# Two-layer attention and expert kernel: batch 1's layer norm, transposes and V matmuls made during batch 0, and GpSimd sums the rotated key in batch 1's first pass

## The reference, cut to what matters

```python
x = x + _layernorm(attn(_layernorm(x)))          # x: (2, 2048, 256), float32
x = x + _layernorm(ffn(_layernorm(x)))
# attn, cut:
xn = x * rsqrt(mean(x * x) + 1e-6) * rms_w
proj = xn @ in_proj_W.T + in_proj_b              # z, K (pairs), V; DI = 512
u = silu(conv4(V) + conv_b)                      # causal, 4 taps, per channel
# per head gates from u: a, w (rotation), beta, r_gate, u_gate, sel_B, sel_C
def step(Sc, inp):                               # scan over the tokens
    Sr = rotate(Sc, a11, a12)
    err = v - sum(k * Sr)
    return Sr + beta * err * k
y = group_norm(sum(Q * Y)) * silu(z) + D * u
return residual + y @ out_W.T
# ffn, cut: a router picks 2 of 8 experts for each batch; gelu(x @ W1 + b1) @ W2 + b2
```

## Time and profile before

| | |
|---|---|
| Median of 3 runs | 1502.98 us (1501.24 to 1503.02) |
| The profiled execution | 1502.64 us, its span 1500.8 us |
| Mean granted TensorE clock | 0.938 |
| PE busy | 1258.7 us (84% of the span), 4244 matmul instructions |
| DVE busy | 1179.0 us (79%), 1933 instructions |
| ACT busy | 516.8 us (34%) |
| POOL busy | 173.9 us (12%), 77 instructions |
| DMA | 98.73 MB, 18.8% of 16 engines' span |

### The profile page before, as it was taken

The page is one execution under the profiler, slowest core; times in us unless marked ns, Lnnn a source line. Parts: engine busy times, 40 slices in busy tenths (PEclk is TensorE's granted clock), DMA queues, the critical chain, the costliest instruction groups (busy, mean ns, idle before and its releaser), DMA issues. The chain is left out here.

```text
span 1500.8 us, 13138 instructions
## 1 busy us (share of the span) xinstructions
PE 1258.7 (84%) x4244; PEld 742.3 (49%) x4244; DVE 1179.0 (79%) x1933; ACT 516.8 (34%) x1186; POOL 173.9 (12%) x77
## 2 busy tenths in 40 slices
PE   5960887773989698895999999899997797999997
PEld 2540333331555455453666666565554474666664
DVE  5889999899999968789899999859999775610011
ACT  3762111000223364666532232321223554332332
POOL 0000244401221200000011111001222100000000
PEclk9985999996999899798999999999999898999999
DMA  4000111100311032200223331312111103432221
GB/s 169 1 8 14 57 52 47 70 1 14 110 45 57 15 118 112 64 8 0 71 84 98 98 98 56 112 70 99 43 57 42 57 1 117 140 133 70 85 70 70
DMA packets 52117, 98.73 MB, mean 66 GB/s; under 512 B 4689, under 2 KB 40018, under 8 KB 50898
## 3 DMA queue, kind: packets, MB, share of 16 engines
q1 hardware_dynamic: 52050, 97.91, 18.8%
HBM read 75.87 MB, written 22.02 MB: 65 GB/s over the span
## 5 line engine op out<-in xcount | busy, mean ns | idle before, releaser
L677 PE MATMUL ps<-kz 128*128 128x256 f32 x1024 | 243.6, 381 | 15.0 <-ACT kz L921 13.3
L663 PE MATMUL ps<-kz 128*128 128x512 f32 x512 | 244.3, 601 | 5.7 <-DVE coef L1110 5.7
L677 PEld LDWEIGHTS ps<-kz 128*128 128x128 f32 x1024 | 195.2, 191 | 98.0 <-issue 60.4
L555 PE MATMUL ps<-wshare,uT 128*128 128x512 f32 x512 | 227.4, 598 | 0.0
L921 ACT ACTIVATE kz<-ps,small 128x512 f32<-128x512 f32 x128 | 87.5, 686 | 302.3 <-PE ps L663 302.1
L477 PE MATMUL ps<-wshare,xnT 128*128 128x512 f32 x256 | 119.3, 610 | 63.4 <-ACT ps L741 63.2
L555 PEld LDWEIGHTS ps<-wshare,uT 128*128 128x128 f32 x512 | 95.9, 192 | 109.8 <-issue 109.8
L663 PEld LDWEIGHTS ps<-kz 128*128 128x128 f32 x512 | 98.5, 193 | 83.0 <-issue 71.4
L975 POOL TENSOR_TENSOR work<-work 128x1024 f32<-128x1024 f32 x28 | 66.8, 2387 | 623.7 <-DVE work L1401 388.3
L823 ACT ACTIVATE kz<-ps 128x128 f32<-128x128 f32 x128 | 33.6, 277 | 288.0 <-PE ps L546 288.0
L1711 DVE TENSOR_TENSOR kz<-ps,b_s 128x256 f32<-128x256 f32 x16 | 6.3, 412 | 135.9 <-PE ps L677 135.9
(11 more groups left out here) (266 smaller groups left out, 2032.3 us busy)
## 6 DMA issues: line engine op xcount, KB each, us to landing
kz<-in_w SPq DMA_DIRECT2D x128, 256.0 KB, 2.9
kap_d<-kz SPq DMA_DIRECT2D x26, 512.0 KB, 2.7
kz<-kap_d SPq DMA_DIRECT2D x26, 512.0 KB, 3.2
uT<-in_x SPq DMA_DIRECT2D x8, 512.0 KB, 5.3
wshare<-in_wq SPq DMA_DIRECT2D x2, 2048.0 KB, 7.8
kz<-in_x SPq DMA_DIRECT2D x2, 2048.0 KB, 8.0
coef<-in_x SPq DMA_DIRECT2D x2, 2048.0 KB, 7.7
wshare<-in_wk SPq DMA_DIRECT2D x2, 1024.0 KB, 11.0
```

The source lines that it names most:

```text
L555: t = mm(ps[:, 2 * (j % 2) + c, :], uT3[:, k, j * P:(j + 1) * P], wq_s[:, k, c, :], start=(k == 0), stop=(k == KI - 1))
L663: t = mm(ps[:, 4 + i % 2, :], w1_r[r][:, k, (f % 2) * P:(f % 2 + 1) * P], x2T[:, k, n * 512:(n + 1) * 512], start=(k == 0), stop=(k == KM ...
L677: t = mm(ps[:, 6 + q // 2, (q % 2) * DM:(q % 2 + 1) * DM], hbuf(i)[:, q * P:(q + 1) * P], w2_r[r][:, f % 2, :], start=(f == 0 and q % 2 == ...
```

## The change

Batch 1's x is loaded at the start into free space (`x_p`). Its statistics and square roots are taken within batch 0's convolution (`x_ahead(0)` to `x_ahead(2)` on DVE, `root_ahead` on ACT), it is scaled on ACT, turned on PE, multiplied with the V weights and evicted on ACT within batch 0's heads (`x_ahead`, `turned_ahead`, `v_ahead`, `values_ahead`). Both results go to DRAM (`store_pre`) and are loaded again for batch 1 (`load_v`, `load_xn`). Batch 1 then has no `normed_x` and no `values`: ACT makes the last tap of 12 tiles from the loaded V (`taps`), DVE that of the other 4. The four banks of the head projections change in batch 1; as a consequence `clean_banks` writes two banks before the first key bias. `expert_weights(0)` comes behind the first 4 tiles of batch 1's convolution, and `x_stats(1)` is gone.

The expert units are shared out anew: 15 ahead of iteration 1 (4 ahead of the head projections, 8 in the heads, 3 behind), 39 in the pass, 10 beside the chunk scan.

In batch 1's first pass GpSimd makes the key sum of i+1 from 2 to 15, and DVE's `rotated(i+1)` within the loop is gone.

```diff
-US, UH = 2, 6
-UNITS = [9] + [9 + 13 * i // 5 for i in range(L - 1)] + [54]
+US, UH = 9, 12
+UF, UM = 4, 7
+UNITS = [15] + [15 + 12 * i // 5 for i in range(L - 1)] + [54]
...
+            def values_ahead():
+                pe.wait_ge(xp_loaded, 16)
+                for i in range(2 * NCH):
+                    n, k = i // 2, i % 2
+                    pe.wait_ge(xnp_ready, 4 * n + 4)
+                    if i >= 4:
+                        pe.wait_ge(xtp_done, i - 3)
+                    for q in range(4):
+                        t = tr(ps[:, 4 + i % 4, q * P:(q + 1) * P], x_p[:, 4 * n + q, k * P:(k + 1) * P], ident[:])
+                    t.then_inc(xtp_ready, 1)
+                for i in range(NV):
+                    n, g = i // KI, i % KI
+                    pe.wait_ge(xtp_done, min(5 + i, 2 * NCH))
+                    if i >= 4:
+                        pe.wait_ge(vp_done, i - 3)
+                    for k in range(KM):
+                        t = mm(ps[:, 4 + i % 4, :], wv_s[:, k, g * P:(g + 1) * P], xnT_p[:, k, n * 512:(n + 1) * 512],
+                               start=(k == 0), stop=(k == KM - 1))
+                    t.then_inc(vp_ready, 1)
...
             for b in range(B):
-                normed_x(b)
-                values(b)
+                if b == 0:
+                    normed_x(b)
+                    values(b)
+                else:
+                    pe.wait_ge(wbc_ready, b)
+                    experts(b - 1, 0, UF)
+                head_projections(b)
                 pe.wait_ge(wk_loaded, b * 16 + 16)
-                head_projections(b)
+                if b > 0:
+                    experts(b - 1, UF, UM)
+                    clean_banks(b)
+                    experts(b - 1, UM, UH)
+                    pe.wait_ge(xnp_loaded, 16)
                 key(b, 0)
                 token_u(b, 0, L - 1)
                 pe.wait_ge(sm_done, b * L + L)
+                if b == 0:
+                    values_ahead()
                 keys(b)
...
                 key_bias(b, 0)
-                for n in range(1, NCH):
-                    silu_u(n)
+                root_ahead(1)
+                silu_u(1)
+                root_ahead(2)
+                silu_u(2)
+                silu_u(3)
...
+                taps(1)
+                experts(b - 1, 0, 2)
+                taps(2)
+                silu_u(0)
+                experts(b - 1, 2, UF)
+                taps(3)
+                silu_u(1)
+                silu_u(2)
+                silu_u(3)
...
                     af(sall[:, 8:11, r], sall[:, 8:11, r], ACT.Sigmoid).then_inc(hd_act, 1)
+                    if b == 0 and h == 0:
+                        x_ahead(0, 5)
+                    elif b == 0:
+                        turned_ahead()
+                        v_ahead(0, 2)
                     act.wait_ge(hd_vec, v0 + 2)
...
             for b in range(B):
                 for i in range(1, L - 1):
+                    if b > 0:
+                        pool.wait_ge(kq_used, 2 * L * b + i + 2)
+                        if i + 1 >= KR1:
+                            pool.wait_ge(k_stored[(i + 1) % KR1], k_stored_count(b, i + 1 - KR1))
+                        nc.gpsimd.tensor_tensor(k1(i + 1), R[:, :, 0], R[:, :, 1], ALU.add).then_inc(k_ready, 1)
                     pool.wait_ge(z1_ready, b * (L - 1) + i)
...
                     t = mark(v.tensor_copy(vbuf[g][:, 0:3, 1:P], vbuf[g][:, L:L + 3, 0:P - 1]))
+                    if b > 0:
+                        t = mark(tsc(acc(0, g), vbuf[g][:, 3:7, :], coeff(g, 3), col[:, C_CB + g:C_CB + g + 1], MUL, ADD))
...
+                if b == 0:
+                    x_ahead(0)
+                else:
+                    expert_weights(b - 1)
                 for n in range(1, NCH):
...
+                    if b == 0 and n < 3:
+                        x_ahead(n)
...
+                if b == 0:
+                    dve.wait_ge(vp_ready, NV)
                 rotate(0, 0)
...
                     at["g"] = mark(tt(g, X[:, :, 0], X[:, :, 1], ADD))
-                    if more and b > 0:
-                        rotated(i + 1)
                     after(at["g"])
```

More of the change, by code:

```diff
@@ L389, in _ @@
                         sp.wait_ge(f_stored, 16 * b)
+                    if b == 0 and j == 5:
+                        sp.wait_ge(pre_stored, 80)
                     if j == 5:
@@ L448, in values, with clean_banks @@
                     t.then_inc(v_ready, 1)
+            def values_ahead():
[17 more added lines that the diff above has]
+                    t.then_inc(vp_ready, 1)
+            def clean_banks(b):
+                pe.wait_ge(sm_done, b * L + L)
+                for c in range(2):
+                    t = mm(ps[:, c, :], ident[:], bk_s[:, 0:512], start=True, stop=True)
+                t.then_inc(bank_ready, 1)
             def head_projections(b):
                 pe.wait_ge(consts_loaded, 16 * 7)
+                pe.wait_ge(wa_loaded, 16 * (b + 2))
                 for j in range(L):
@@ new lines, in x_ahead, with turned_ahead @@
+            def x_ahead(first, last):
+                act.wait_ge(pre_vec, 3)
+                for j in range(first, last):
+                    af(x_p[:, j], x_p[:, j], ACT.Identity, scale=t2[:, j:j + 1], bias=t0[:, j:j + 1]).then_inc(xnp_ready, 1)
+            def turned_ahead():
+                for i in range(2 * NCH):
+                    n, k = i // 2, i % 2
+                    act.wait_ge(xtp_ready, i + 1)
+                    af(xnT_p[:, k, n * 512:(n + 1) * 512], ps[:, 4 + i % 4, :], ACT.Copy,
+                       scale=col[:, C_RMS + k:C_RMS + k + 1]).then_inc(xtp_done, 1)
@@ new lines, in v_ahead, with taps_and_u, taps, silu_u @@
+            def v_ahead(first, last):
+                for i in range(first, last):
+                    g = i % KI
+                    act.wait_ge(vp_ready, i + 1)
+                    af(v_p(i), ps[:, 4 + i % 4, :], ACT.Identity, bias=col[:, C_BV + g:C_BV + g + 1]).then_inc(vp_done, 1)
+            def taps_and_u(b):
+                def taps(n):
+                    for g in range(KI):
+                        act.wait_ge(vp_loaded[g], 16)
+                        af(uT3[:, g, n * 512:(n + 1) * 512].rearrange("p (j c) -> p j c", c=P),
+                           vbuf[g][:, 3 + 4 * n:7 + 4 * n, :], ACT.Identity,
+                           scale=col[:, C_CW + 4 * g + 3:C_CW + 4 * g + 4], bias=col[:, C_CB + g:C_CB + g + 1]
+                           ).then_inc(tap1_ready, 1)
+                def silu_u(n):
+                    for g in range(KI):
+                        act.wait_ge(conv_done, b * NV + n * KI + g + 1)
+                        ug = uT3[:, g, n * 512:(n + 1) * 512]
+                        af(ug, ug, ACT.Silu).then_inc(u_ready, 1)
+                taps(1)
[7 more added lines that the diff above has]
+                silu_u(3)
```

171 lines of the change are left out of this document (135 added, 36 removed).

## The result

The changed kernel takes **1514.41 us** (median of 4 runs, 1513.80 to 1514.91) against 1502.25 us of the kernel before beside it: ratio 1.0084, 95% interval 1.0071 to 1.0096. It is slower by 12.2 us; 1514.4 us was forecast. The profiled execution took 1513.91 us, with a span of 1512.0 us against 1500.8.

What follows compares the result with a forecast made beforehand. DVE was taken to set the pace of batch 1's first pass, PE 0.2 us behind. Terms 14.4 - 16.0 + 7.0 + 6.4 = +11.8 us on the profiled 1502.64 gave 1514.4 us, range 1500 to 1528.

Steps and rivals of the forecast that it cites:

- The forecast's own case: Whole kernel: slower, 1514.4 us, own range 1504 to 1526, chance 0.72.
- 1. Key sum: Batch 1's first pass: GpSimd's key sum holds DVE's outer product, +1.03 us in each of 14 iterations, +14.4 us.
- The reading from iteration 15: Old trace, batch 1's first pass: outer product behind POOL's sum took 4.32 us for 2.28, expected in every changed iteration.
- free sum: Rival, batch 1's first pass: GpSimd's sum holds nothing and PE binds at 12.14 us per iteration; 1488 us, chance 0.14.
- One sign: Batch 1's first pass: PE would show 1.9 us of idle per iteration.
- 2. Batch 1's start: From batch 1's start into its heads: DVE loses statistics, scaling and the V wait; -16.8 to the heads, -16.0 us net.
- The wait before the first head tile: Batch 1's start: DVE idle near 12 us ahead of the first head tile, ended by PE.
- 3. Convolution: Batch 0's convolution: added statistics on DVE and a 4.2 us wait for ACT's first root, +7.0 us.
- 4. Batch 0's heads: Batch 0's heads, second half: DVE waits for squares (+4.4) and Sqrt (+2.0) behind added ACT and PE work, +6.4 us.
- cold V chain: Rival, batch 0's heads: V tiles run at the 1.2 GHz level, 3.66 us each, delaying DVE; 1539 us, chance 0.05.

Runs made afterwards that it cites:

- e1: Changed kernel with the rotated key's sum of batch 1's first pass back on DVE, between g and the outer product: 1500.62 us.
- e2: Kernel before with only the key sum of batch 1's first pass moved to GpSimd: 1516.89 us against 1502.97.
- e3: Changed kernel with GpSimd's key sum released only by the end of the outer product: 1516.73 us.
- e9: Changed kernel with DVE's value(i+1) of batch 1's first pass, large input in PSUM, moved between g and the outer product: 1508.51 us.
- e5: Changed kernel with the key sum on DVE and batch 1's head projections ahead of all expert units on PE: 1487.13 us.
- e7: Changed kernel with the key sum on DVE and the two roots in batch 0's convolution one tile later: 1494.14 us.
- e6: Changed kernel with the key sum on DVE, batch 0's added work reordered in convolution and heads, and batch 1's head projections first: 1477.01 us.
- e8: Changed kernel with half of each key sum on GpSimd and the other half on DVE ahead of g: 1511.75 us.

## Why the prediction was right

The forecast's own case (chance 0.72), its sign and its range held. That 1514.4 us agrees with the median to a hundredth is luck: the working gave +11.8 from the profiled execution's 1502.64, and measured were +12.2 by the medians and +11.2 by the spans. The terms, one by one:

- **1. Key sum, +14.4.** By the two traces the pass from its first to its last state product grew by 13.1 + 1.3 = 14.4 us; by the runs it is 13.8 (`e1`) and 13.9 (`e2`). The reading from iteration 15 was right in each piece: 4.33 us, POOL's 3.26, a period near 14.05. The rival "free sum" fell with `e2`, and with `e3` and `e9` also the idea that the outer product is special or that any DVE operation is held. One sign came smaller than foretold: PE was idle for 15.3 us of the 196.8 between the first and the last state product, 1.1 us per iteration instead of 1.9, at a granted clock of 0.97 where it had been 1.00 and never idle. The rule of the Trainium skill ("SBUF — State Buffer", section "Who interferes with whom"), that the later of two such instructions is held until the other is through, agrees in every run with a hold: 2.04, 2.16, 0.97 and 1.55 us.
- **2. Batch 1's start, -16.0.** -15.8 up to the heads (-16.8 forecast), and +0.6 from there to the first pass (+0.8 forecast): -15.2. The wait before the first head tile came at its place, ended by PE, at 14.08 for 12 us; `up(0)` and `up(1)` took 6.41 us there. `e5` shows that the term's cause, four units ahead of the projections, was named rightly.
- **3. Convolution, +7.0.** +6.6, with 4.45 us of wait for the first root (4.2 forecast). `e7` gives back 4.5 of it.
- **4. Batch 0's heads, +6.4.** +6.4 by the distance (heads +6.6, first pass +13.0), 6.2 by the waits: 4.0 for the squares (4.4 forecast), 1.8 less the old 0.4 for the second half's Sqrt (2.0 forecast), and 0.7 for the first half's Sqrt, which I had at 0. The way to the 4.4 came as worked out. Of the eight groups of transposes PE made four early, and the other four, then the V tiles, stood behind ACT's first copy at 120.20:

```profile
110.96 3.67 PE L510 MATMUL ps<-ident,kz 128*128 128x128 f32 x16 [7.63 <-DVE coef L1322]
121.01 3.65 PE L510 MATMUL ps<-ident,kz 128*128 128x128 f32 x16 [6.38 <-ACT kz L887]
124.45 28.33 PE L518 MATMUL ps<-kz,wshare 128*128 128x512 f32 x64
```

PE did come out cold: the granted clock was 0.50 (the 1.2 GHz level) from 110 to 124.4 us, and the four groups took 3.65 us where they would have been 2.4 at full clock. ACT took the second V tile at 128.78, 8.6 us after its first copy began, where I had 9.2 (112.8 to 122.0); the eviction and the squares then took 1.4 (to 130.16) for 1.2. Together that is the 4.0 for 4.4.
- **What had no term.** Batch 0's first pass ran 0.9 us longer. DVE waited 5.3 us in it for PE where it had waited 4.1. The granted clock over its first 44 us was 0.88 (156 to 200 us) for 0.89 (143 to 187), so that is not the difference. From the first to the last state product it is 144.3 us for 143.0 before, 143.1 in `e1` and 144.5 in `e7`: it comes and goes, and why stays open. Behind batch 1's first pass DVE waited 5.6 instead of 6.9 us for PE. By the terms as measured it is 14.4 - 15.2 + 6.6 + 6.2 = 12.0, with these two 11.6, against +11.2 of the spans.

The cold V chain (1539) did not come, though its condition was there at the start: the clock was 0.50 up to 124.4 us and 1.00 from 126 on, 1.6 us into the chain, which then kept it. A V tile took 1.77 us over the whole chain, not 3.66. From 100 to 150 us the granted clock was 0.80, where it had been 0.52 with PE nearly idle.

## What to carry to other kernels

An idle GpSimd is no free engine. If DVE comes to an operation with two SBUF inputs while a GpSimd sum that reads SBUF is running, DVE pays what is left of that sum, less what it was spared. Here that was 2.04 us for 1.02 (the removed sum's slot of 1.14, less the 0.12 by which g's slot grew). The sum should stand beside DVE operations that read PSUM: `e9` put one of 0.68 us there and got 5.9 us back. No run here covered the whole sum in that way, so that such a move pays is not shown. Look in the old trace for one iteration that already has the new meeting; iteration 15 gave the term to within 0.6 us. And where work is moved into an engine's gaps, its place in that engine's list, relative to what another engine waits for, was worth 24 us here by the medians (`e1` to `e6`; 21 by the profiled executions) with the same instructions.

## What the hardware showed that I had not expected

- The hold can be counted to a few hundredths. It is what is left of GpSimd's instruction when the DVE operation starts, less 0.12 to 0.14 us, whatever the operation:

| Held operation | left of GpSimd's row, us | held, us |
|---|---|---|
| g, `e9` | 0.29 | 0.16 |
| outer product, `e8` | 1.09 | 0.97 |
| product of 512 columns, before | 1.68 | 1.55 |
| outer product, `e9` | 1.69 | 1.55 |
| outer product, changed kernel | 2.18 | 2.04 |
| subtraction, `e3` | 2.29 | 2.16 |

The hold is the duration less the free one: 1.22 us for g, 2.28 for the outer product and the subtraction, and 0.69 for 512 columns (L1535, just ahead of that product). A DVE operation with one PSUM input ran at its 0.68 us in the middle of the key sum (`e9`).

- It works the other way too. The key sum started when g had 1.05 us to run (801.66 to 802.71) and took 0.91 more than the 2.35 that such a sum takes alone.
- The wait hides in the duration of the held instruction, on POOL as on DVE: the key sum's row of 3.26 us (2.35 alone) began while g was still running, and in `e3`'s iteration the Z product. No idle time stands before it, so a view of waits shows nothing.
